# Local attention before a two-layer network: grouping by batch, conditioning as small matrices, score sums in column strips, fewer operations a step

## The reference, cut to what matters

```python
q  = (x @ WQ_w + WQ_b).reshape(8, 256, 16, 64)      # 16 heads of 64
k  = (x @ WK_w + WK_b).reshape(8, 256, 16, 64)
ak = (ax @ WK_w + WK_b).reshape(8, 1, 16, 64)       # ax: conditioning, one row a batch
av = (ax @ WV_w + WV_b).reshape(8, 1, 16, 64)
k_shift = stack([k at l-1, k at l, k at l+1])       # zero outside the sequence
K = concat([ak, k_shift]);  V = concat([av, k_shift])      # the local values are the keys
scores = einsum('blhd,blhjd->blhj', q, K) / sqrt(64)
alphas = softmax(scores, axis=-1)                   # over 4 entries
att = einsum('blhj,blhjd->blhd', alphas, V).reshape(8, 256, 1024)
return att @ WO_w + WO_b
```

## Time and profile before

| what | value |
|---|---|
| profiled execution's own time | 1703.39 us |
| its span (first to last instruction) | 1701.6 us |
| TensorE busy / share of span | 1564.6 us / 92% |
| VectorE busy | 827.5 us / 49% |
| ScalarE busy | 662.9 us / 39% |
| mean granted TensorE clock | 0.942 |
| local attention: cond projections to the last `yB` | 13.4 to 370.9 us |
| linear attention | 371.9 to 568.9 us |

### The profile page before, as it was taken

How to read it: one execution, slowest core, us unless ns; L and a number is a source line. 1 busy time by engine, 2 the same in 40 slices (tenths; PEclk the granted TensorE clock), 3 DMA queues, 4 the chain that set the end, 5 groups by cost and what they waited for, 6 DMA issues and landing times. The chain is left out here.

```text
span 1701.6 us, 32009 instructions
## 1 busy us (share of the span) xinstructions
PE 1564.6 (92%) x11861; PEld 1250.0 (73%) x11862; DVE 827.5 (49%) x2926; ACT 662.9 (39%) x2449; POOL 94.7 (6%) x135
## 2 busy tenths in 40 slices
PE   7999989879999899999999999879999999866995
PEld 5666555537777799999999999638888888753663
DVE  2777668755445334444444444473333333565223
ACT  3211112125555145555555455314344434523442
POOL 0000000000000000000000000010000000003662
PEclk9988889889999999999999999859999999967998
DMA  4000000000000300000000000010000000001113
GB/s 146 1 1 1 0 1 1 1 0 1 1 1 1 100 1 2 2 1 2 2 2 1 2 2 1 1 31 21 20 26 20 27 14 2 1 1 47 41 43 92
DMA packets 27731, 28.05 MB, mean 16 GB/s; under 512 B 2293, under 2 KB 22234, under 8 KB 27450
## 3 DMA queue, kind: packets, MB, share of 16 engines
q1 hardware_dynamic: 20970, 16.70, 3.4%
q0 software_dynamic: 2496, 5.12, 1.0%
q10 hardware_dynamic: 4112, 4.19, 0.8%
HBM read 21.35 MB, written 4.65 MB: 15 GB/s over the span
## 5 line engine op out<-in xcount | busy, mean ns | idle before, releaser
L1457 PE MATMUL spare<-identb 128*128 128x128 bf16 x3166 | 218.2, 219 | 0.0
L1457 PEld LDWEIGHTS spare<-identb 128*128 128x128 bf16 x3166 | 201.7, 103 | 4.3
L292 PE MATMUL sc<-headsel,prod 128*128 128x128 f32 x1024 | 164.6, 315 | 0.7 <-DVE prod L437 0.7
L292 PEld LDWEIGHTS sc<-headsel,prod 128*128 128x128 f32 x1024 | 142.6, 218 | 26.7 <-issue 24.3
L1055 DVE TENSOR_TENSOR_SCAN narg<-rz,pre_n 128x16 f32<-128x16 f32 x256 | 47.9, 187 | 219.9 <-PE pre_n L952 218.9
L990 ACT ACTIVATE ghid<-gh_ps,cols 128x128 f32<-128x128 f32 x512 | 144.3, 366 | 12.9 <-PE gh_ps L891 12.7
L891 PE MATMUL gh_ps<-hist,w 128*128 128x128 f32 x1024 | 137.5, 275 | 0.6 <-ACT ghid L990 0.6
L900 PE MATMUL gy_ps<-w2e,ghid 128*128 128x128 f32 x1024 | 136.8, 276 | 0.6
L900 PEld LDWEIGHTS gy_ps<-w2e,ghid 128*128 128x128 f32 x1024 | 124.4, 191 | 3.0 <-issue 3.0
L891 PEld LDWEIGHTS gh_ps<-hist,w 128*128 128x128 f32 x1024 | 126.0, 188 | 0.8 <-DVE hist L1063 0.8
L952 PE MATMUL pre_r<-hist,gru_w 128*128 128x128 f32 x512 | 118.1, 312 | 0.7 <-DVE hist L1063 0.5
(11 more groups left out here) (374 smaller groups left out, 2664.1 us busy)
## 6 DMA issues: line engine op xcount, KB each, us to landing
w<-in_L_ffn_W SPq DMA_DIRECT2D x1, 2048.0 KB, 9.6
raw<-in_L_ffn_wg SPq DMA_DIRECT2D x8, 256.0 KB, 2.9
raw<-in_L_ffn_wu SPq DMA_DIRECT2D x8, 256.0 KB, 2.8
raw<-in_L_ffn_wd SPq DMA_DIRECT2D x8, 256.0 KB, 2.7
wqkv<-in_L_attn_Wqkv SPq DMA_DIRECT2D x1, 1536.0 KB, 6.4
mrow<-mt SPq DMA_DIRECT2D x4, 256.0 KB, 2.4
y_top<-yrow SPq DMA_DIRECT2D x4, 256.0 KB, 5.4
y_next<-yrow ACTq DMA_DIRECT2D x4, 256.0 KB, 6.1
```

What stands on the lines that cost most here:

```text
L292: mm = nc.tensor.matmul(sc[:, :, :, :].rearrange("p i j h -> p (i j h)"), prod[u % 2][:, j, P * i:P * i + P], headsel[:, P - 2 * k:2 * P - ...
L1457: nc.tensor.matmul(spare[:, 0:P], n.identb[:, :], n.identb[:, :], start=True, stop=True)
```

## The change

The stage is cut otherwise. Tokens stay batch-major in a new buffer `xB`, which `setup` writes contiguously in place of `xT`, and which `linear_attention`'s `add` (L766) reads for the residual sum when it writes `xT`. Two batches make a group of W = 512 tokens, four groups times eight chunks make 32 steps s. The conditioning entry j = 0 leaves the per-token products: its score is x times a small matrix made once (`gq`: WQ's chunk transposed, times the conditioning key, 8 matmuls, with a bias part `gcol`), two matmuls a group (`cond_scores`), and its value enters as a second small matrix (`av_wo`: conditioning value times WO) with two matmuls a group. Three local entries remain (J = 3), whose products come from one VectorE operation a step on an overlapping view of `kb`. The score sums are the other way round: `headsel` with 32 columns is stationary, the product is moving, and entry j adds up on PSUM partitions 32(j+1) to 32(j+1)+31 over all eight chunks of a group. So softmax runs once a group for 16 heads, on 128 x 256, after ScalarE has copied the sums and TensorE has turned them. Of the three terms only two are added on VectorE (`pair`); the third goes into PSUM by a matmul of its own. The value side runs LAG = 10 steps behind. `turn_probs` makes 8 bfloat16 transposes (96 and 48 columns) and 4 float32 ones of the conditioning entry's probability. VectorE's ten softmax operations are the ones of before, one function each (`soft_max` to `part_low`), with the product by the reciprocal in two.

```diff
@@ setup
-                    out = n.xT[:, :].rearrange("p (i t b) -> p b i t", i=2, b=B)[:, 2 * g:2 * g + 2]
-                    nc.scalar.activation(out, turn[g % 2][:, :, :].rearrange("p (b i) t -> p b i t", i=2),
+                    nc.scalar.activation(n.xB[:, 512 * g:512 * g + 512], turn[g % 2][:, :, :].rearrange("p i t -> p (i t)"),
                                          ACT.Copy).then_inc(x_kept, 1)
@@ local_attention, sizes
-    UNITS = 2 * NC
-    J = 4
+    J = 3
+    GB = 2
+    W = GB * T
+    NG = B // GB
+    STEPS = NG * NC
+    LAG = NC + 2
+    NK = LAG + 2
+    R = 32
+    HR = HEADS
...
+        kb = sb("kb", [P, NK, GB, T + 2])
+        prod = [sb(f"prod{i}", [P, J, W]) for i in range(2)]
...
+        pj = [ps(f"pj{i}", [P, W]) for i in range(2)]
+        bc = [ps(f"bc{i}", [P, W]) for i in range(2)]
+        sc = ps("sc", [P, W])
+        y_ps = ps("y_ps", [P, W])
+        tok = ps("tok", [P, W])
+        tr = ps("tr", [2 * 3 * HR, 2, W], BF16)
@@ gpsimd: nine selects of 96 x 1024 instead of three of 24 x 512
+                pool.memset(pick[:, :, :, :, :], 0.0).then_inc(const_a, 1)
...
+                        pool.affine_select(out=pick[:, j, :, :, :], in_=pick[:, j, :, :, :], compare_op=ALU.not_equal,
...
@@ tensor
+                def scores(s, j):
...
+                    if j == 0 and c == 0 and g >= 1:
+                        pe.wait_ge(sc_kept, GB * g)
+                    if j == 0:
+                        pe.wait_ge(prod_v, s + 1)
+                    at = R * (j + 1)
+                    mm = nc.tensor.matmul(sc[at:at + R, :], headsel[:, R - 2 * c:2 * R - 2 * c], prod[s % 2][:, j, :],
+                                          start=(c == 0), stop=(c == NC - 1))
...
+                def cond_scores(g):
...
+                        mm = nc.tensor.matmul(sc[0:R, T * i:T * i + T], gq[:, b, :], n.xB[:, T * b:T * b + T],
+                                              start=(i == 0), stop=(i == GB - 1))
+                    mm.then_inc(group_scored, 1)
...
+                def turn_scores(g):
+                    pe.wait_ge(sc_kept, GB * (g + 1))
...
+                    for i in range(4):
+                        mm = nc.tensor.transpose(tok[:, P * i:P * i + P], sc_sb[:, P * i:P * i + P], n.ident[:, :])
+                    mm.then_inc(sc_turned, 1)
...
+                def turn_probs(g):
+                    pe.wait_ge(parts_done, g + 1)
...
+                def spread_probs(u, j):
...
+                    if j == 0 and c == 0:
+                        pe.wait_ge(turned_kept, g + 1)
...
+                    if k >= 2:
+                        pe.wait_ge(term_done, k - 1)
+                    k0 = 2 * 3 * HR if j < 2 else 3 * HR
+                    nc.tensor.matmul(bc[k % 2][:, :], pick[0:k0, j, c, :, :].rearrange("r h d -> r (h d)"),
+                                     probT[0:k0, j // 2, :], start=True, stop=True).then_inc(spread, 1)
...
+                def project_out(u):
...
+                    pe.wait_ge(term_done, J * (u + 1))
+                    nc.tensor.matmul(y_ps[:, :], wo[:, c, :], term[u % 2][:, J - 1, :], start=False, stop=False)
+                    pe.wait_ge(pair_done, u + 1)
+                    nc.tensor.matmul(y_ps[:, :], wo[:, c, :], pair[u % 2][:, :], start=False,
+                                     stop=(c == NC - 1)).then_inc(y_part, 1)
+
                 pe.wait_ge(cond_kept, 2)
+                project(0, 0)
+                project(0, 1)
+                turn_wq(0)
+                project(1, 0)
+                turn_wq(1)
+                project(1, 1)
+                pe.wait_ge(cond_split, 2)
                 pe.wait_ge(const_done, 2)
...
+                for s in range(STEPS + LAG + 1):
+                    u = s - LAG
+                    project(s + 2, 0)
+                    spread_probs(u, 0)
+                    project(s + 2, 1)
+                    spread_probs(u, 1)
+                    project_out(u - 1)
+                    spread_probs(u, 2)
+                    if s == 1:
+                        cond_values()
+                    if s == 2:
+                        cond_keys()
+                    if s == 3:
+                        turn_cond_values(0)
+                        cond_bias()
+                    if s == 4:
+                        turn_cond_values(1)
+                    if s % NC == 0 and 1 <= s // NC <= NG:
+                        turn_scores(s // NC - 1)
+                    scores(s, 0)
+                    scores(s, 1)
+                    scores(s, 2)
+                    if s % NC == NC - 1 and s < STEPS:
+                        cond_scores(s // NC)
+                    if s % NC == 1 and 1 <= s // NC <= NG:
+                        turn_probs(s // NC - 1)
@@ scalar
+                for s in range(STEPS + LAG + 1):
+                    after, at = divmod(s, NC)
+                    if at == 0 and 1 <= after <= NG:
+                        keep_scores(after - 1)
+                    if at == 2 and 1 <= after <= NG:
+                        keep_turned(after - 1)
+                    keep_projections(s + 2)
...
+                    if at == 0 and 1 <= after <= NG:
+                        exps(after - 1)
+                    if s >= LAG + NC and (s - LAG) % NC == 0:
+                        keep_y((s - LAG) // NC - 1)
@@ vector
+                def product(s):
...
+                    one = kb[:, s % NK, :, 0:T]
+                    three = bass.AP(one.tensor, one.offset, [one.ap[0], (1, J), *one.ap[1:]])
+                    q = qb[s % 3][:, :].rearrange("p (b t) -> p b t", b=GB).unsqueeze(1).broadcast_to([P, J, GB, T])
+                    nc.vector.tensor_tensor(prod[s % 2][:, :, :].rearrange("p j (b t) -> p j b t", b=GB), q, three,
                                             ALU.mult).then_inc(prod_v, 1)
...
+                product(0)
+                for s in range(STEPS + LAG + 1):
+                    u = s - LAG
...
+                    if split:
+                        soft_sum(g)
+                    weighted(u, 0)
+                    if split:
+                        soft_reciprocal(g)
+                    weighted(u, 1)
+                    if split:
+                        soft_scale(g)
+                    product(s + 1)
+                    if split:
+                        part_high(g)
...
+                    if g is not None and at == 0:
+                        soft_max(g)
+                    weighted(u, 2)
+                    if split:
+                        part_rest(g)
+                        part_middle(g)
+                    if g is not None and at == 0:
+                        soft_shift(g)
+                    pair_terms(u)
+                    if split:
+                        part_last(g)
+                        part_low(g)
```

More of the change, by code:

```diff
@@ L187, in local_attention @@
         bq8 = sb("bq8", [P, NC])
-        headsel = sb("headsel", [P, 2 * P])
-        pick = sb("pick", [24, J, 2, HD], BF16)
+        headsel = sb("headsel", [P, 2 * R])
+        pick = sb("pick", [2 * 3 * HR, J, NC, 2, HD], BF16)
         akT, avT = sb("akT", [P, NC, B]), sb("avT", [P, NC, B])
[L194 to L204, removed]
@@ new lines, in turn_wq, with cond_values @@
+                def turn_wq(half):
+                    for i in range(4):
+                        c = 4 * half + i
+                        mm = nc.tensor.transpose(bc[half][:, P * i:P * i + P], wq[:, P * c:P * c + P], n.ident[:, :])
+                    mm.then_inc(wq_turned, 1)
+                def cond_values():
+                    for c in range(NC):
+                        mm = nc.tensor.matmul(y_ps[:, 16 * c:16 * c + 16], wo[:, c, :],
+                                              avZ[:, c, :, :].rearrange("p b h -> p (b h)"), start=True, stop=True)
+                    mm.then_inc(wav_done, 1)
@@ new lines, in cond_keys @@
+                def cond_keys():
+                    pe.wait_ge(wq_kept, 2)
+                    for c in range(NC):
+                        rhs = akZ[:, c, :, :].rearrange("p b h -> p (b h)")
+                        nc.tensor.matmul(tok[:, 16 * c:16 * c + 16], wqT[:, c, :], rhs, start=True, stop=True)
+                        mm = nc.tensor.matmul(tok[0:1, P + 16 * c:P + 16 * c + 16], n.cols[:, ROWS["bq"][0] + c:ROWS["bq"][0] + c + 1],
+                                              rhs, start=True, stop=True)
+                    mm.then_inc(gq_done, 1)
@@ new lines, in turn_cond_values, with cond_bias @@
+                def turn_cond_values(half):
+                    if half == 0:
+                        pe.wait_ge(wav_kept, 1)
+                        pe.wait_ge(wq_kept, 2)
+                    for i in range(4):
+                        b = 4 * half + i
+                        mm = nc.tensor.transpose(bc[half][0:HEADS, P * i:P * i + P], wavT[:, b, :], n.ident[:, :])
+                    mm.then_inc(av_turned, 1)
+                def cond_bias():
+                    pe.wait_ge(gq_kept, 1)
```

(24 more changed lines are left out.)

459 lines of the change are left out of this document (229 added, 230 removed).

## The result

The changed kernel took 1579.76 us (median; 1573.92 to 1581.07), the kernel before 1703.15 us in the same comparison: ratio 0.9276, 95% interval 0.924 to 0.9311. The profiled execution took 1581.07 us with a span of 1579.0 us. The last `yB` ends at 249.45 us, 370.9 before: 121.4 us less. What follows took 1329.6 us where it took 1330.7. So the whole gain lies in the stage, as forecast, and so does nearly all of the error.

What follows compares the result with a forecast made beforehand. The prediction took TensorE to bound the stage, VectorE second. Start, steps, small matrices, group waits, clock and tail summed to a stage end of 281.6 us, 89.3 less than before: forecast 1614 us, range 1582 to 1660.

Steps and rivals of the forecast that it cites:

- the price of the score matmuls: TensorE's step: three score matmuls in strips overlap partly, four record times of six, 1.71 us (bounds 0.86 and 2.57).
- rival of more overlap: Score matmuls: strips overlap more than the 1.71 us a step assumed; 1588 us, chance 0.17.
- The price from the Trainium skill: Score matmuls: three column strips 2.38 times as fast as in a row, an estimated 1.08 us a step, 1594 us.
- The spread matmuls of 96 rows: TensorE's step: three spread matmuls at 0.31 us each, 0.93 us, with 0.2 a step for changes of shape.
- The small matrices: Made on TensorE's path for the conditioning entry: 10.7 us, bounds 7 and 16.
- `cond_scores`, charged 3.4 us: Conditioning score matmuls: four records of 256 columns a group, 0.86 us, four times 3.4 us.
- the group waits with their clock: Softmax once a group: 4.0 us for group 0, 5.3 for groups 1 and 2, plus 7.5 for the lower clock.
- the wait at `part_low`: TensorE waits 2.2 us a group for VectorE's softmax, 0.9 in group 0; this can bring the lower clock.
- The tail: Steps 32 to 42 and `yB`: three softmax steps, then seven of 3.8 us at clock 0.76; 45.7 us.
- The clock rivals: Changed stage: clock falls often in the loop, 1635 us, chance 0.07; strips keep it low, slower than before, 0.03.
- the sign of 0.95: Sign that the forecast is right: TensorE's clock above 0.95 in 85 to 235 us.
- slower than before: Rival: strips keep the stage's clock at the lower level; near 1815 us at 0.50 throughout, chance 0.03.

Runs made afterwards that it cites:

- the last two versions: Changed kernel with later value side, ordered transposes and third spread matmul first in the tail: 1568.13 us; the same plus third term on VectorE in 20 steps: 1571.96 us.
- the run in which the tail kept its matmul and its clock: Changed kernel with the third term added on VectorE only in the first 20 steps of the value side, while projections run: 1581.4 us.
- the last version: Changed kernel with later value side, ordered transposes, third term on VectorE in the first 20 steps and third spread matmul first in the tail: 1571.96 us.

## Why the prediction was wrong

**The step that failed** is the price of the score matmuls: "entry j+1's first record can start with entry j's second one ... four record times of six", 1.71 us. The records come in rounds, all first ones together, then all second ones: 0.99 us, two record times and a change of shape. 32 x 0.72 = 23 us of the 32.2 by which the stage's end was missed. The mechanism was right in kind, strips side by side, and wrong in the order of the records; what made it wrong was the assumption that the next matmul's first record has to wait for the start of the second record of the one ahead. The run with a fourth strip refutes that (0.99 us again, not 0.43 more), and the one with a strip used twice shows that two matmuls of one strip are what cannot share. The prediction's rival of more overlap is the case that came; its 1588 us is 8 us too long because of the terms below. The price from the Trainium skill, TensorE: Matmul & The Clock Gate, Part 3: Packing small matmuls (2.38 times for three strips), gave an estimated 1.08 us a step; here 2.68 / 0.99 is 2.7 times, and the measured value stands.

**The other terms.** The spread matmuls of 96 rows had no changeover: with 0.22 for two of three, the rest of the step is 4.39 us where 4.57 were charged, 4.0 us over the 22 middle steps. The small matrices took 6.9 us (starts at 31.39 to 33.17, 35.98 to 39.41, 42.22 to 43.34 and 46.15 to 46.68 us), not 10.7, in which the last 32 records, 3.1, would have been 4.0 at the 0.124 us of the others. `cond_scores`, charged 3.4 us, is free: it lies in the fourth strip beside the score records (its step, 53.47 to 56.39, is as long as its neighbour, 50.57 to 53.47). The loop started 1.2 us earlier, and the group waits with their clock cost some 2 us less than charged. With the scores that is 37 to 38 us, more than the miss, because two things were charged at nothing:

```profile
76.04 1.12 PE L283 MATMUL pj<-xB,wk 128*128 128x512 f32 x2 [1.19 <-ACT kb L457]
...
129.14 1.13 PE L396 MATMUL y_ps<-p0T,av_wo 16*128 16x256 f32 x4
```

The matmuls that bring the conditioning value into `y_ps`, two a group, are in no term of the sum. They cost 1.25 us with their changes of shape (the step with them, 126.79 to 133.42, is 6.63 us long, the next 5.38), 3.7 us in steps 10 to 31 and once more in the tail. And TensorE waits 1.2 us for `kb` in step 11. With the tail's 1.1 us, in which the fourth group's matmuls are, the miss closes to within 1 us. So the near agreement of the middle steps' group terms (18.2 us charged, 19.5 measured above the plain step) is partly luck: a term that is free was charged, one that costs was forgotten.

That the small matrices cost 6.9 us holds for this profile. In the profiles of four other versions with the same instructions there (the transposes by shape and the product as three operations, each alone, and the last two versions) the step between the score matmuls of steps 2 and 3 is 6.7 us instead of 3.9. In that of the transposes by shape the clock falls to 0.50 (42 to 44 us) with TensorE busy without a gap from 34 us on. This moves the stage's end by some 3 us with no edit behind it.

**What held.** VectorE behind TensorE in the middle; the product at 1.75 us, and no gain from its being one operation; the wait at `part_low`, 2.55 us against 2.2, with the lower clock after it (0.50 while the transposes of group 1 ran). A step with such a wait is 10.8 us long (109.09 to 119.92), 5.5 more than a plain one. The tail came to 46.8 us against 45.7, but by other numbers: 3.2 us a step at clock 1.00, not 3.8 at 0.76, and more at group 3's softmax, where TensorE waits 3.6 us and the clock is 0.54 from 212 to 223 us. The clock rivals did not come: in steps 10 to 31, each with its strips, the clock was 0.95, and 0.93 from 85 to 235 us, a little under the sign of 0.95 that the prediction set. (The 1815 us of "slower than before" is not its own sum: 1614 + 225, less some 14 already charged for the clock, is near 1825.) The low clock in the tail of the run with the third term on VectorE is no case of that rival, as no strips run there. What follows the stage did not move by more than 1.1 us in all.

## What to carry to other kernels

Here float32 matmuls with 32 stationary columns and 512 moving ones, whose outputs lie in different strips of 32 partitions, cost as much as one for up to four (0.99 us), if they stand next to each other in TensorE's order; a lone one costs no less (0.98). Count changes of shape between neighbouring matmuls, and order equal ones together. When a step waits for a chain that comes once a group, read where TensorE stands still, and move the consumer back by one step before making the chain shorter; the clock that the wait costs comes on top. When a sum comes out, go through the instructions once more for those that stand in no term. And before a difference of a few us between two profiles is explained, look whether it is there already ahead of the edit.

## What the runs showed of the hardware that was not expected

- Float32 records of several strips run in rounds: four start within 20 ns, the second four 0.45 us later.
- Fewer matmuls can be slower: with one 512-column matmul less a step in the tail and one addition more, the granted clock was 0.55 from 205 to 262 us and a step took 4.8 us instead of 3.2. No run takes the addition and the clock apart; that most of it is the clock's is the estimate above (1.3 of 1.6 us), together with the middle of the same run (5.1 us at 1.00) and the run in which the tail kept its matmul and its clock. How TensorE's activity is judged the runs don't tell.
- After the same wait of 2.55 us the clock was down when the transposes began in group 1, and in group 2 of the same profile only after their 1.41 us; and in the profile of the transposes by shape it fell with no wait ahead, while the small matrices were made.
- Alternating bfloat16 transposes of 96 and 48 columns take 0.18 us each at clock 1.00 (1.41 for eight) and 0.25 at 0.50 (2.02); in order 0.09 at 1.00 (0.69) and 0.14 at 0.50 (1.11, group 3 of the last version).
